# Alternating select banks, and a gather tile of every fifth chunk fetched row by row by SyncE, in a graph-attention kernel

## What is computed

```python
h  = relu(layernorm(x))                                  # 12500 x 32
xl = einsum('ni,nio->no', h, hetero_w[node_type]) + hetero_b[node_type]
x_i, x_j = xl[dst], xl[src]                              # per edge
ete = lrelu(edge_type_emb[edge_type]);  eae = lrelu(edge_attr @ edge_attr_w)
alpha = lrelu(concat([x_i, x_j, ete, eae]) @ att_w)
alpha = softmax of alpha over the edges with the same dst
msg   = concat([x_j, eae]) @ lin_w * alpha
out   = x + segment_sum(msg, dst)
```

## Time and profile before

| what | value |
|---|---|
| median of three timed runs | 3364.27 us (3363.03 to 3402.62) |
| the profiled execution's own time | 3359.11 us |
| its span in the trace | 3356.9 us |
| mean granted TensorE clock | 0.968 of full speed |
| instructions in the trace | 66,615 |

### The profile page before, as it was taken

How to read it: one execution, slowest core, us unless ns; L and a number is a source line. 1 busy time by engine, 2 the same in 40 slices (tenths; PEclk the granted TensorE clock), 3 DMA queues, 4 the chain that set the end, 5 groups by cost and what they waited for, 6 DMA issues and landing times.

```text
span 3356.9 us, 66615 instructions
## 1 busy us (share of the span) xinstructions
PE 3034.6 (90%) x21526; PEld 2581.3 (77%) x21526; DVE 2951.4 (88%) x7259; ACT 896.6 (27%) x2095; POOL 2489.4 (74%) x2630
## 2 busy tenths in 40 slices
PE   7999999999999999999999999999999999999910
PEld 5788888877878888878878878878888888888710
DVE  9889999988989989989889898899889898998836
ACT  4222232322322322222223223223222232232200
POOL 4777777777777777777777777777777777777756
PEclk8999999999999999999999999999999999999965
DMA  5233333333333333333333333333333333334523
GB/s 194 70 76 93 74 94 74 90 78 74 93 75 74 93 74 78 90 74 88 80 74 90 78 74 93 75 74 94 74 76 92 74 83 85 74 89 110 123 76 81
DMA packets 186497, 287.58 MB, mean 86 GB/s; under 512 B 73986, under 2 KB 141274, under 8 KB 185500
## 3 DMA queue, kind: packets, MB, share of 16 engines
q1 hardware_dynamic: 77084, 165.53, 16.2%
q0 software_dynamic: 84768, 52.50, 13.6%
q10 hardware_dynamic: 24288, 64.79, 5.4%
HBM read 210.11 MB, written 72.48 MB: 84 GB/s over the span
## 4 chain that ended last, share of the span: by engine, by line
POOL 31%; PE 26%; DVE 22%; issue 18%; DMA 3%; POOLq 0%; DVEq 0%; ACT 0%; SPq 0%; ACTq 0%
POOL gath L623 28%; PE ps_misc L888 20%; DVE sel_a L1174 8%; PE ps_pick L902 3%; DVE gath L1198 2%; DVE sel_b L1174 2%; DMA gath<-table_dram,meta 2%; DVE dscore L1206 2%; PE ps_misc L890 1%; PE ps_attr L912 1%; DVE slot_a L1180 1%; POOL hib L665 1%; DVE ps_msg L1280 1%; DVE ps_misc L1245 1%; POOL node_buf L665 1%
## 5 line engine op out<-in xcount | busy, mean ns | idle before, releaser
L623 POOL DMA_INDIRECT gath<-table_dram,meta x2500 | 2366.8, 947 | 792.7 <-issue 746.1
L888 PE MATMUL ps_misc<-parts,sel_a 128*128 128x462 f32 x5250 | 1217.1, 383 | 85.9 <-DVE gath L1198 85.9
L888 PEld LDWEIGHTS ps_misc<-parts,sel_a 128*128 128x128 f32 x5250 | 973.5, 191 | 204.9 <-DVE gath L1198 103.6
L888 PE MATMUL ps_misc<-parts,sel_b 128*128 128x462 f32 x3500 | 805.2, 381 | 28.2 <-DVE gath L1198 24.8
L888 PEld LDWEIGHTS ps_misc<-parts,sel_b 128*128 128x128 f32 x3500 | 644.0, 189 | 117.4 <-DVE gath L1198 44.4
L902 PE MATMUL ps_pick<-s_dst,onehot 122*128 122x128 bf16 x9375 | 652.5, 220 | 51.7 <-issue 22.8
L902 PEld LDWEIGHTS ps_pick<-s_dst,onehot 122*128 122x128 bf16 x9375 | 539.6, 98 | 198.2 <-issue 152.2
L1198 DVE TENSOR_REDUCE gath<-ps_misc 128x33 f32<-128x462 f32 x625 | 392.0, 627 | 154.2 <-PE ps_misc L890 154.1
L1206 DVE TENSOR_REDUCE dscore<-ps_pick 128x4 f32<-128x512 f32 x875 | 521.2, 618 | 3.0 <-PE ps_pick L902 3.0
L775 ACT ACTIVATE wts<-args 128x50 f32<-128x50 f32 x125 | 30.8, 246 | 1685.7 <-DVE args L1303 1685.7
L1174 DVE TENSOR_SCALAR sel_a<-dst_f,part_group 128x384 fp32r<-128x384 f16 x875 | 465.3, 603 | 0.0
(11 more groups left out here) (244 smaller groups left out, 1866.1 us busy)
## 6 DMA issues: line engine op xcount, KB each, us to landing
hib<-digit_dram SPq DMA_DIRECT2D x125, 612.5 KB
rows_dram<-rows ACTq DMA_DIRECT2D x125, 437.5 KB
gath<-table_dram,meta POOLq DMA_INDIRECT x2500
attr<-edge_attr_t_in SPq DMA_DIRECT2D x125, 200.0 KB
dst_f<-sel_code_dram SPq DMA_DIRECT2D x125, 160.0 KB
hib<-digit_dram SPq DMA_DIRECT2D x250, 50.0 KB
rows_dram<-no_rows ACTq DMA_DIRECT2D x1, 8575.0 KB, 42.9
hib<-digit_dram SPq DMA_DIRECT2D x250, 25.0 KB
```

The source lines that it names most:

```text
L623: nc.gpsimd.indirect_dma_start(gath[u][:, t, :], None, table_dram, bass.IndirectOffsetOnAxis(ap=meta_sb[u][:, t:t + 1], axis=0)).then_inc( ...
L888: nc.tensor.matmul(ps_sel, rows_of[:, g, at, 0:P], parts[:, k, g, :], start=(g == 0 and k == 0), stop=False)
```

## The change

The selects of a chunk alternate between the two banks of `ps_misc`. The sum of `TS_OF` is 25, odd, so `BANK_OF` is (0, 0, 0, 0, 0) and the banks in a chunk are 0, 1, 0, 1, 0. A select then waits for the take two before it, except the first of a chunk, which uses the bank of the chunk before's last. To free bank 1, `terms` moves to SBUF.

Tile `ROW_T` = 19 of the first chunk (u = 0) of every iteration but the first is no longer gathered by POOL. SP loads the 128 source numbers of that tile (`row_src`) into `row_ids` during the first chunk of the iteration before. Then, in each of the first four chunks of that iteration, behind the ordinary loads, it reads 32 of them into registers, four at a time, and issues one DMA for every row. Each of the four steps has a semaphore of its own, `row_landed`. DVE waits for all four ahead of line 1280 of the first chunk.

```diff
+BANK_OF = tuple(sum(TS_OF[0:u]) % 2 for u in range(U)) if sum(TS_OF) % 2 == 0 else (0,) * U
+ROW_T = T - 1 - TS_OF[0]
+ROW_STEPS = 4
+ROWS_EACH = P // ROW_STEPS
...
+        row_ids = hi_f[32:33, slot_at:slot_at + P].bitcast(i32)
...
-        ps_sel = ps_misc[:, 0, 0:VW * GN]
-        terms = ps_misc[:, 1, 0:HALF * (T + 1)].rearrange("p (f t) -> p f t", t=T + 1)
+        terms = sb("terms", [P, HALF, T + 1])
...
+        def ps_sel(u, j):
+            return ps_misc[:, (BANK_OF[u] + j) % 2, 0:VW * GN]
+        def read(n):
+            return n + 2
+        def same_bank(u, j):
+            return j == 0 and (BANK_OF[u] + TS_OF[u - 1] - 1 + BANK_OF[u - 1]) % 2 == 0
...
+            def fetch_rows(k):
+                for first in range(k * ROWS_EACH, (k + 1) * ROWS_EACH, 4):
+                    nodes = [sp.value_load(row_ids[:, r:r + 1], min_val=0, max_val=N_NODES - 1)
+                             for r in range(first, first + 4)]
+                    for r, node in enumerate(nodes, first):
+                        sp.dma_start(gath[0][r:r + 1, ROW_T, :], table_dram[ds(node, 1), :]).then_inc(
+                            row_landed[k], 16)
             with sp.Fori(0, ITERS - 1) as i:
                 for u in range(U):
                     c = i * U + u
                     sp.wait_ge(sums_ready, count(c + 1))
+                    if u == 0:
+                        sp.dma_start(row_ids, row_src[ds(i + 1, 1), :]).then_inc(row_src_in, 16)
                     load_hib(c + HIB_AHEAD, (u + HIB_AHEAD) % U)
...
                     load_attr(c + U, u)
+                    if u == 0:
+                        sp.wait_ge(row_src_in, (i + 1) * 16)
+                        sp.sem_inc(row_turns, 1)
+                    if u < ROW_STEPS:
+                        fetch_rows(u)
...
-                    gather_chunk(i, u, False, T - TS_OF[u])
+                    gather_chunk(i, u, False, T - TS_OF[u] - (u == 0))
...
-                pe.wait_ge(sel_read, count(selected(i, u) + j))
+                pe.wait_ge(sel_read, read(selected(i, u) + j - (0 if same_bank(u, j) else 1)))
...
-                    dve.wait_ge(gathered[u], (i + 1) * (16 * (T - TS_OF[u])))
-                    dve.wait_ge(sel_read, count(selected(i, u) + TS_OF[u]))
+                    dve.wait_ge(gathered[u], (i + 1) * (16 * (T - TS_OF[u] - (u == 0))) + 16 * (u == 0))
+                    if u == 0:
+                        for k in range(ROW_STEPS):
+                            dve.wait_ge(row_landed[k], count(i * (16 * ROWS_EACH)))
+                    dve.wait_ge(sel_read, read(selected(i, u) + TS_OF[u]))
```

More of the change, by code:

```diff
@@ L72, with gnn_kernel @@
 MB = N7 * N_NODE_TYPES
-def gnn_kernel(nc, x, meta, dst_rows, dst_tmajor, type_tmajor, sel_src, row_edges, row_last, edge_attr_t, node_type,
+def gnn_kernel(nc, x, meta, dst_rows, dst_tmajor, type_tmajor, sel_src, row_edges, row_last, row_src, edge_attr_t, node_type,
                hetero_wT, hetero_bT, edge_type_emb, edge_attr_w, att_w, lin_w, out):
@@ L360, in gnn_kernel @@
         gathered = [sem(f"gathered{u}") for u in range(U)]
+        row_src_in = sem("row_src_in")
+        row_turns = sem("row_turns")
+        row_landed = [sem(f"row_landed{k}") for k in range(ROW_STEPS)]
         stored = [sem(f"stored{u}") for u in range(U)]
@@ L433, in _ @@
         def _(sp):
+            start_at_one(sp, *row_landed)
             def load_hib(c, u):
@@ L630, in _ @@
                 for u in range(U):
-                    gather_chunk(i, u, False, T - TS_OF[u])
+                    gather_chunk(i, u, False, T - TS_OF[u] - (u == 0))
             for u in range(U):
-                gather_chunk(ITERS - 1, u, False, T - (TS_OF[u] if u < U - 1 else TS_LAST))
+                gather_chunk(ITERS - 1, u, False, T - (TS_OF[u] if u < U - 1 else TS_LAST) - (u == 0))
             flag = is_unsorted(pool)
@@ L884, in select @@
                 rows_of, slots_of, at = (sel_a, slot_a, j) if j < TS_A else (sel_b, slot_b, j - TS_A)
-                pe.wait_ge(sel_read, count(selected(i, u) + j))
+                pe.wait_ge(sel_read, read(selected(i, u) + j - (0 if same_bank(u, j) else 1)))
                 for g in range(NG):
                     for k in range(2):
-                        nc.tensor.matmul(ps_sel, rows_of[:, g, at, 0:P], parts[:, k, g, :],
+                        nc.tensor.matmul(ps_sel(u, j), rows_of[:, g, at, 0:P], parts[:, k, g, :],
                                          start=(g == 0 and k == 0), stop=False)
-                nc.tensor.matmul(ps_sel, slots_of[:, at, 0:P], slot_pen[:].rearrange("p f n -> p (f n)"),
+                nc.tensor.matmul(ps_sel(u, j), slots_of[:, at, 0:P], slot_pen[:].rearrange("p f n -> p (f n)"),
                                  start=False, stop=True).then_inc(sel_mm, 1)
@@ L940, in count_falls @@
                 pe.wait_ge(falls_ready, 1)
-                pe.wait_ge(sel_read, count(SELECTED))
+                pe.wait_ge(sel_read, read(SELECTED))
                 nc.tensor.matmul(ps_misc[:, 0, 0:1], before_me[:], falls[:, 0:1], start=True, stop=True).then_inc(
@@ L1010, in _ @@
             start_at_one(dve, eae_ready, signs_summed, picked, msg_added, msg_used, sums_ready, sel_read)
+            dve.sem_inc(sel_read, 1)
             steps = [0]
@@ L1197, in take @@
                 dve.wait_ge(sel_mm, count(selected(i, u) + j + 1))
-                v.tensor_reduce(gath[u][:, T - 1 - j, 0:VW], ps_sel.rearrange("p (f n) -> p f n", n=GN), AX.X,
+                v.tensor_reduce(gath[u][:, T - 1 - j, 0:VW], ps_sel(u, j).rearrange("p (f n) -> p f n", n=GN), AX.X,
                                 ALU.max).then_inc(sel_read, 1)
@@ L1273, in chunk @@
                     dve.wait_ge(gathered[u], 16 * ((T - TS_OF[u]) * ITERS + TS_OF[u] - TS_LAST))
-                    dve.wait_ge(sel_read, count(SELECTED))
+                    dve.wait_ge(sel_read, read(SELECTED))
                 else:
-                    dve.wait_ge(gathered[u], (i + 1) * (16 * (T - TS_OF[u])))
-                    dve.wait_ge(sel_read, count(selected(i, u) + TS_OF[u]))
+                    dve.wait_ge(gathered[u], (i + 1) * (16 * (T - TS_OF[u] - (u == 0))) + 16 * (u == 0))
[3 more added lines that the diff above has]
+                    dve.wait_ge(sel_read, read(selected(i, u) + TS_OF[u]))
                 dve.wait_ge(msg_mm, count(c + 1))
@@ L1638 @@
     sel = src.reshape(P, CHUNKS, T)[:, :, :T - 1 - TS:-1]
+    row_src = src.reshape(P, ITERS, U * T)[:, :, ROW_T].T
     arrays = {
@@ L1647 @@
         "row_last_in": rows[:, -1],
+        "row_src_in": row_src,
         "edge_attr_t_in": attr.reshape(G * F_EDGE, CHUNKS, TG * P),
```

## The result

The changed kernel takes 4423.0 us (median of 4 runs, 4420.0 to 4455.2) against 3365.2 us: ratio 1.313, 95% interval 1.302 to 1.324. Slower by 1058 us, where the forecast was 4946 us within 3700 to 5350. The profiled execution has a span of 4418.5 us against 3356.9.

What follows compares the result with a forecast made beforehand. POOL's gathers were taken to bound the kernel; SP's rows would take over, 190.4 us an iteration, 65.9 more, +1582 us over 24 iterations. 3359.1 + 1582 = 4941, median 5 above: 4946 us, range 3700 to 5350.

Steps and rivals of the forecast that it cites:

- POOL paces before, SP after: POOL's gathers, one every 1.25 us, set the pace before; SP's 128 rows, 157.4 us an iteration, set it after.
- signs named: Trace marks of being right: loads near 0.47 us, steps some 40, DVE idle some 35, few sums waits, POOL waiting for DVE.
- The ring: Circle of waits from DVE's scan through SP's rows back to the scan: 190.4 us an iteration, 65.9 more than now.
- Landing: The last row's DMA lands some 2 us after its issue; only then does line 1280 start.
- The row: SP's cost for one row: load with checks 0.80 us plus DMA with address 0.43, together 1.23 us.
- My lower end: Low end of the main forecast's own range: a row of 1.01 us, giving 4270 us.
- Overlapping loads: Rival: SP's loads overlap in fours, 0.86 us a row, 3794 us; overlapping or cheaper loads, 3500 to 4270, have 0.15.
- Late hib adds 0: `hib` loads issued behind SP's rows come about 15 to 20 us late; DVE would wait anyway, so 0.
- Two banks 0, bounds 0 and -105: PE loses most of its 105.4 us of waits for the take before, worth 0 while something slower paces.
- Terms in SBUF, -12 to +24: DVE's writes to SBUF: half a microsecond gained to one lost a chunk, -12 to +24 us in all, taken as 0.
- The contention rival: SP keeps up, but scans reading two SBUF tensors block POOL's gathers: 3394 to 3559 us; chance half of 0.10.
- lower of my two rates: Line 1158's rate of scans blocking gathers: 0.25 us each, ten scans an iteration cost POOL 2.5 us; 3394 us.

Runs made afterwards that it cites:

- rows-alone kernel: The changed kernel with the selects back in one bank and the terms in PSUM, SP still fetching rows: 4444 us, ratio 1.323 to the kernel before.
- the terms alone: The kernel before with one edit, the scan's terms in SBUF; no rows fetched by SP, selects in one bank: 3422 us, ratio 1.018.
- with two banks: The kernel before with the terms in SBUF and the selects in two banks, without SP's rows: 3443 us, ratio 1.026.

## Why the prediction was right, and where its size was off

- *POOL paces before, SP after.* Right: SP's wait for the sums fell from 2421.6 to 172.9 us, and 65% of the chain is SP's queue. Of the signs named, the steps (38.7 us for 40), DVE's stop ahead of the row addition (27 us for 35, with a stop for `hib` before it) and POOL's waiting for DVE came; the loads near 0.47 us did not.
- *The ring.* Right in shape: steps, landing, first chunk, once an iteration. Kernels that shortened SP's part moved the time by 24 times that: 830 us for 835 without the checks, 213 for 225 with `hib` on ACT. Landing was 1.2 us for 2, the chunk behind it 11.5 for 11.0.
- *The row, the step that was mis-sized.* "I take 0.80 for one" `value_load`, from line 428's single execution. It was 0.63. Line 428's load stands alone, and 0.80 is what the first load of a group costs; the three behind it cost 0.55 to 0.56 each, and I took the price of the first for all four. 0.17 x 128 x 24 = 522 us, and 4946 - 522 = 4424. The DMA's 0.43 held to the hundredth, in part by luck: it came from DMAs of 277 ns with an address step of 37, and a row's has 225, with a step of 42 and a move of 29. My lower end, 1.01 us a row, had a cheaper load and a cheaper check in it and counted for 4270; the true 1.06 lay near it.
- *Overlapping loads* did not occur: three loads in a group are cheaper, but each waits for the check and the assert before it, and the time without checks fell by their whole length. The Trainium skill (DMA: Bandwidth & Descriptors, Latency and other measured facts) gives a floor of about 600 ns for a register load; the median here is 268 ns, and the first of a group has 518, so the measurement decides.
- *Late hib adds 0.* Right: 20.8 us an iteration of waits, worth nothing when removed. In the iteration shown DVE's two waits are 6 and 14 us, where I had 15 to 20 each.
- *Two banks 0, bounds 0 and -105.* Right for the change as it stands, as far as its runs tell. Without the rows they cost 21 us, outside my bounds: I had not thought that they could lose. "DVE or the rows would be late next" was right: PE's wait moved to the picks.
- *Terms in SBUF, -12 to +24.* A write of line 1286 takes 548 ns. The rows-alone kernel, with the terms in PSUM, has the same four writes a chunk at

```profile
L1285 DVE TENSOR_TENSOR ps_misc<-ps_msg,wts 128x240 f32<-128x240 f32 x500 | 159.4, 365 | 0.2 <-ACT wts L815 0.2
```

  so they lose 0.73 us a chunk, more than the half microsecond that I allowed. In the ring only one chunk of five counts, 24 x 0.73 = 18 us, inside the bound on the time. The pair of kernels with and without it is too close to show them (4423 and 4444 us).
- *The contention rival* was not the outcome, but its mechanism is real near the lower of my two rates: 0.25 us a scan forecast, 62.8 us over 250 scans, 0.25, measured with the terms alone, and 0.34 with two banks (84.5 us). With SP out of the way it turns a gain of 29 us into a loss of 44 to 48.

## What to carry to other kernels

A queue that "idles" can take work only to the length of its own step: price each moved item by its sequencer instructions (load, check, address, DMA), in the number in which they come, and compare step with chunk too, not only sum with iteration. A single record of an instruction gives its price in its place: one load alone costs what the first of a group costs, and those behind it cost less. A wait that is taken away may come back on another line; look for it there before counting it as gained. And a gain of one gather in a hundred is lost at once if the same edit gives two SBUF operands to a scan that runs beside the engine that sets the pace.

## What the runs showed of the hardware

- One load instruction for 16 row numbers took 3.52 us from one place and 1.23 us 8 bytes further on.
- A range check behind a load, with its assert and gaps, cost SP 0.27 us a row, as much as a load that follows another. The first load of a group took 518 ns, the next three 262 to 274.
- With both inputs of a scan in SBUF, a gather that starts while it runs took 1.21 us on average; longer by the rest of the scan less 0.19 us; one that starts before the scan and runs into it took 0.94, as without a scan.
- PE's granted clock was 0.86 over the iteration shown of the changed kernel, a mean between its two levels (1.2 and 2.4 GHz), with PE busy 122.65 of 168 us. PE waits there for DVE, which waits for `hib` and then for the rows: the clock was 0.59 from 1760 to 1780 us, with PE busy 6.14 us. It was 1.00, the upper level, with 759.52 of 800 busy:

```profile
1649.00:1817.00 168.00, 122.65 (x848) 106.00 (x848) 114.91 (x282) 34.28 (x81) 96.36 (x100) 0.86 0.26 61
...
1760.00:1780.00 20.00, 6.14 (x32) 5.24 (x32) 2.97 (x5) 0.00 (x0) 6.52 (x7) 0.59 0.26 68
```
